# Token rows of expert slots: fetched by index in the experts' loop, not scattered beforehand

## The reference, cut to what matters

```
probs = softmax(flat @ router_w.T)                 # 4096 x 8
topk_probs, topk_idx = top_k(probs, 2)             # two experts for each token
gates = topk_probs / (sum + 1e-9)
h = silu(x @ w1[e].T) * (x @ w3[e].T)              # 341 wide, for the token's two experts
out[n] = sum over its two experts: gate * (h @ w2[e].T)
```

## Time and profile before

| | |
|---|---|
| profiled execution, its own time | 2860.51 us |
| span from first to last instruction | 2858.6 us |
| mean granted TensorE clock | 0.899 of full speed |
| TensorE busy | 2337.6 us (82%), 16656 instructions |
| GpSimd busy | 537.8 us (19%), 575 instructions |
| `route_block` | 2473.7 to 2635 us of the span |
| `experts_block` | 2636.0 to the end |

### The profile page before, as it was taken

One profiled execution on the slowest core, in us unless ns is written; L12 is line 12 of the kernel. 1 busy time (PEld: TensorE's weight loads), 2 busy tenths in 40 slices (PEclk: granted clock), 3 DMA queues, 4 the chain that ended last, 5 costly groups with the idle time before them and its releaser, 6 DMA issues. The chain is left out here.

```text
span 2858.6 us, 46600 instructions
## 1 busy us (share of the span) xinstructions
PE 2337.6 (82%) x16656; PEld 1554.2 (54%) x16656; DVE 1682.3 (59%) x3155; ACT 1215.4 (43%) x2665; POOL 537.8 (19%) x575
## 2 busy tenths in 40 slices
PE   5585867763899999799999799999899999620995
PEld 3354545542566666466566466666566665310884
DVE  4767676764366566366566365665465664550676
ACT  2343333430455555355455355555355555410442
POOL 0133333352011011011011010110010110235332
PEclk8787887885999999899999899999899999755997
DMA  2254545478647546455655465565466461431113
GB/s 94 99 212 164 189 182 196 171 284 204 138 96 145 126 97 138 106 126 109 127 125 119 91 132 125 114 130 117 105 139 125 97 145 37 127 58 52 46 52 108
DMA packets 222862, 360.74 MB, mean 126 GB/s; under 512 B 68794, under 2 KB 124701, under 8 KB 222240
## 3 DMA queue, kind: packets, MB, share of 16 engines
q1 hardware_dynamic: 218304, 349.20, 48.8%
q0 software_dynamic: 4320, 8.43, 0.9%
HBM read 229.58 MB, written 126.56 MB: 125 GB/s over the span
## 5 line engine op out<-in xcount | busy, mean ns | idle before, releaser
L1400 ACT ACTIVATE prob<-ps 128x512 f32<-128x512 f32 (+5 forms) x1600 | 636.5, 441 | 733.5 <-PE ps L1351 587.7
L1453 DVE TENSOR_REDUCE maxima<-ps 128x1 f32<-128x512 f32 (+3 forms) x768 | 387.7, 547 | 293.7 <-PE ps L1279 146.5
L1372 PE MATMUL ps<-prob,plain 128*32 128x512 f32 (+5 forms) x3200 | 512.0, 443 | 0.0
L1423 POOL TENSOR_TENSOR products<-products,sums 128x256 f32<-128x256 f32 x192 | 140.3, 731 | 1604.5 <-DVE sums L1444 1603.2
L1458 DVE TENSOR_REDUCE maxima<-ps 128x2 f32<-128x512 f32 (+1 forms) x512 | 294.2, 608 | 242.9 <-PE ps L1290 99.7
L1444 DVE RECIPROCAL sums<-sums 128x256 f32<-128x256 f32 x192 | 331.5, 1736 | 103.9 <-ACT sums L1411 103.9
L1343 PE MATMUL ps<-q1a_s,k1a_s 128*128 128x512 f32 (+3 forms) x768 | 303.4, 395 | 0.0
L1351 PE MATMUL ps<-q1b_s,k1b_s 128*128 128x512 f32 (+3 forms) x768 | 301.3, 393 | 0.0
L1372 PE MATMUL ps<-prob,v_s 128*32 128x512 f32 (+3 forms) x1536 | 284.4, 491 | 0.0
L1279 PE MATMUL ps<-k1a_s,q1a_s 128*128 128x512 f32 (+3 forms) x768 | 234.4, 375 | 2.8 <-DMA k1a_s<-k1ah_dram 2.8
L1343 PEld LDWEIGHTS ps<-q1a_s,k1a_s 128*128 128x128 f32 x768 | 147.4, 192 | 126.8 <-issue 118.9
(11 more groups left out here) (332 smaller groups left out, 4837.1 us busy)
## 6 DMA issues: line engine op xcount, KB each, us to landing
qh_dram<-pairs SPq DMA_DIRECT2D x96, 512.0 KB, 3.3
kwh_dram<-pairs SPq DMA_DIRECT2D x64, 512.0 KB, 3.0
qa_s<-qh_dram SPq DMA_DIRECT2D x128, 256.0 KB, 4.5
kwa_s<-kwh_dram SPq DMA_DIRECT2D x128, 256.0 KB, 7.4
q1a_s<-qh_dram SPq DMA_DIRECT2D x128, 256.0 KB, 4.7
qb_s<-qh_dram SPq DMA_DIRECT2D x64, 256.0 KB, 9.0
kwb_s<-kwh_dram SPq DMA_DIRECT2D x64, 256.0 KB, 9.9
k1a_s<-k1ah_dram SPq DMA_DIRECT2D x32, 512.0 KB, 6.9
```

The costliest lines, as they stand in the source:

```text
L1372: mm = pe.matmul(ps[at:at + VD, SCORES + k % 2, q0 - c * CH:q0 - c * CH + w], w_, m.prob[:, n % PROBS, h, 0:w], start=first, stop=True, sk ...
L1400: act.activation(m.prob[:, u % PROBS, h, 0:w], ps[:, turn % SCORES, 0:w], ACT.Exp, scale=SCALE).then_inc(s["exp_done"], 1)
L1423: pool.tensor_tensor(o, o, m.sums[:, br, cc], ALU.mult).then_inc(s["divided"], 1)
L1453: ins = dve.tensor_reduce(partial[:, h, i, part:part + 1], bank[:, 0:w], AX, ALU.max)
```

## The change

The place of each pair is found as before. The scatter is gone, and with it the zeros, the second copy of the tokens and the index column (rows are now 128 wide). SP stores the normalised tokens once, in token order, in eight DMAs of 256 KB as they become ready. Small tables grow by `lanes` and `edges`, and `token` holds float numbers, one more than the pair's.

What is needed instead is the inverse: for each place, its pair. The kernel forms `behind[pair, s]` = (slot of pair >= 128 s) for s = 0..71 (64 tiles of pairs, 4608 elements a partition), sums it to get the tile number and so the lane (slot mod 128), forms a one-hot `at_lane[pair, lane]`, multiplies `behind` by the pair's number, and adds up `at_lane^T x behind` over the 64 tiles on TensorE. The difference of neighbouring columns is the number of the pair at that lane of slot s. It works in four quarters of 16 tiles:

```diff
+            for q in range(QUARTERS):
+                pe.wait_ge(s["lanes_done"], q + 1)
+                pe.wait_ge(s["named_done"], q + 1)
+                for n in range(q * PAIRS_OF // QUARTERS, (q + 1) * PAIRS_OF // QUARTERS):
+                    mm = pe.matmul(ps[:, 7, 0:SLOTS + 1], at_lane[:, n % TILES_OF, :], behind[:, n, :], start=n == 0,
+                                   stop=n == PAIRS_OF - 1)
+                mm.then_inc(s["found_done"], 1)
...
             for g in range(groups):
                 act.wait_ge(s["back"], g + 1)
                 act.copy(xf[:, g * CH:(g + 1) * CH], ps[:, 2 + g % 2, :]).then_inc(s["back_copied"], 1)
+                if g == 1:
+                    act.wait_ge(s["w_loaded"], 48)
+                if g in (1, 3):
+                    k = g // 2
+                    act.copy((m.w1, m.w3)[k][0][:].rearrange("p e n -> p (e n)"), raw[k]).then_inc(s["w_hi"], 1)
...
-            pool.wait_ge(s["placed"], 1)
-            for t in range(TILES_OF):
-                for k in range(2):
-                    pool.indirect_dma_start(m.xs, bass.IndirectOffsetOnAxis(ap=where[:, k, t:t + 1], axis=0),
...
+            for k, (hi, lo) in enumerate((m.w1, m.w3)):
+                pool.wait_ge(s["w_hi"], k + 1)
+                pool.tensor_tensor(lo[:].rearrange("p e n -> p (e n)"), raw[k],
...
+            for q in range(QUARTERS):
+                pool.wait_ge(s["behind_done"], 2)
+                pool.tensor_tensor(behind[:, qq, :], behind[:, qq, :], each_tile(token[:, qq], SLOTS + 1), ALU.mult)\
+                    .then_inc(s["named_done"], 1)
+            pool.wait_ge(s["w_hi"], 3)
+            pool.tensor_tensor(m.w2[:, :, :, 1, :], raw[2].rearrange("p (e k n) -> p e k n", e=NE, k=KH),
...
```

VectorE, behind `slot` (left out between the last two: six more operations on 71 columns, which give the rows to store to, `m.put`):

```diff
+            dve.wait_ge(s["w_lo"], 2)
+            dve.tensor_tensor(behind, each_tile(slot[:], SLOTS + 1), each_token(edges[:], PAIRS_OF), ALU.is_ge)\
+            dve.tensor_reduce(tile_no[:], behind, AX, ALU.add).then_inc(s["behind_done"], 1)
+            run(dve.tensor_scalar(tile_no[:], tile_no[:], -float(P), float(P), ALU.mult, ALU.add))
+            run(dve.tensor_tensor(lane[:], slot[:], tile_no[:], ALU.add))
+            for q in range(QUARTERS):
+                if q >= 2:
+                    dve.wait_ge(s["found_done"], q - 1)
+                dve.tensor_tensor(at_lane[:, q % 2 * n:(q % 2 + 1) * n, :], each_tile(lane[:, qq], P), each_token(lanes[:], n), ALU.is_equal)\
...
+            dve.wait_ge(s["found_done"], QUARTERS)
+            run(dve.tensor_copy(found[:], ps[:, 7, 0:SLOTS + 1]))
...
+            dve.tensor_scalar(m.get[:], place_of[:], 0.0, None, ALU.max)
```

The low parts of the weights move from VectorE to GpSimd; `behind` lies in the memory of the raw weights w1 and w3, so that VectorE waits for their low parts. In the experts' block SP's loads of `xin` go, and GpSimd issues both the fetch of the rows and the store:

```diff
+            def get(g):
+                if g >= 3:
+                    pool.wait_ge(s["x_ready"], g - 2)
+                for n, i in enumerate(tiles(g)):
+                    at = bass.IndirectOffsetOnAxis(ap=m.get[:, i:i + 1], axis=0)
+                    pool.indirect_dma_start(m.xin[:, g % 3, n, :], None, m.xs, at, bounds_check=B * T - 1, oob_is_err=False)\
+                        .then_inc(s["in%d" % (g % 3)], 16)
+
+            for g in range(2):
+                get(g)
             for i in range(SLOTS):
+                if i % GROUP == 0 and i // GROUP + 2 < loads:
+                    get(i // GROUP + 2)
                 pool.wait_ge(s["y_done"], i + 1)
-                at = bass.IndirectOffsetOnAxis(ap=m.xin[:, g % 3, i % GROUP, P:ROW].bitcast(I32), axis=0)
+                at = bass.IndirectOffsetOnAxis(ap=m.put[:, i:i + 1], axis=0)
```

More of the change, by code:

```diff
@@ L1532, in route_block @@
     above = sb("above", [P, SLOTS, NE], F32)
-    slot = sb("slot", [P, 2, TILES_OF], F32)
-    where = sb("where", [P, 2, TILES_OF], I32)
+    slot = sb("slot", [P, PAIRS_OF], F32)
+    behind = raw_13[:, 0:PAIRS_OF * (SLOTS + 1)].rearrange("p (n s) -> p n s", n=PAIRS_OF)
+    tile_no, lane = [sb(n, [P, PAIRS_OF], F32) for n in ("tile_no", "lane")]
+    at_lane = t2[:].rearrange("p b (n q) -> p (b n) q", q=P)
+    lanes = sb("lanes", [P, P], F32)
+    edges = sb("edges", [P, SLOTS + 1], F32)
+    found = sb("found", [P, SLOTS + 1], F32)
+    place_of, spare = [sb(n, [P, SLOTS], F32) for n in ("place_of", "spare")]
     owner_f = sb("owner_f", [P, SLOTS], F32)
     stack = ExitStack()
-    s = open_sems(nc, stack, "w_loaded t_loaded0 t_loaded1 t_loaded2 t_loaded3 small_loaded empty_set cleared w_hi "
+    s = open_sems(nc, stack, "w_loaded t_loaded0 t_loaded1 t_loaded2 t_loaded3 small_loaded w_hi w_lo "
                              "turned t_copied stats aggregated std_done xn_done back back_copied logits_done shifted "
-                             "exp_done chosen_done counted placed scattered chain id_done copied ones_set")
+                             "exp_done chosen_done counted behind_done named_done lanes_done found_done kept chain ones_set")
     groups = TILES_OF // GROUP
@@ L1552, in _ @@
             for k, name in enumerate(("w1", "w3", "w2")):
[L1553 to L1557, removed]
+                sp.dma_start(raw[k], d[name]).then_inc(s["w_loaded"], 16)
+            for g in range(groups):
+                sp.wait_ge(s["xn_done"], GROUP * (g + 1))
+                rows = m.xs[GROUP * g * P:GROUP * (g + 1) * P]
+                sp.dma_start(rows.rearrange("(t p) n -> p t n", p=P), xn[:, GROUP * g:GROUP * (g + 1), :])\
+                    .then_inc(s["kept"], 16)
+            sp.wait_ge(s["kept"], 16 * groups)
             sp.wait_ge(s["w_loaded"], 48)
@@ L1613, in _ @@
-            pool.memset(empty[:, P:ROW].bitcast(I32), 2 * B * T).then_inc(s["empty_set"], 1)
-            pool.wait_ge(s["small_loaded"], 16 * 6)
-            for k in range(2):
[L1616 to L1620, removed]
@@ L1729, in experts_block @@
     loads = -(-SLOTS // GROUP)
-    m.xin = sb("xin", [P, 3, GROUP, ROW])
+    m.xin = sb("xin", [P, 3, GROUP, P])
     m.xh = sb("xh_t", [C, 2, CH], F32R)
@@ L1749, in tiles, with rows_in @@
         return range(GROUP * g, min(GROUP * (g + 1), SLOTS))
+    def rows_in(g):
+        return sum(len(tiles(x)) for x in range(g % 3, g + 1, 3))
     def puts_before(i, k):
@@ L1757, in _ @@
         def _(sp):
[L1758 to L1766, removed]
             for k in range(4):
@@ L1788, in turn_x @@
                 for i in range(len(tiles(g))):
-                    mm = pe.transpose(ps[:, 7, i * P:(i + 1) * P], m.xin[:, g % 3, i, 0:P], m.ident[:])
+                    mm = pe.transpose(ps[:, 7, i * P:(i + 1) * P], m.xin[:, g % 3, i, :], m.ident[:])
                 mm.then_inc(s["x_ready"], 1)
```

70 lines of the change are left out of this document (35 added, 35 removed).

## The result

The changed kernel took 2892.61 us (median of 4 runs, 2890.21 to 2895.0) against 2861.78 us (2857.88 to 2863.4) for the kernel before: ratio 1.011, 95% interval 1.0092 to 1.0127. That is slower, where 2835 us was predicted. Run again later, word for word, it took 2851.27 us (2846.49 to 2855.57) beside 2861.22 us: ratio 0.9958, interval 0.9945 to 0.9971, which is faster; and a third time 2893.7 us. The experiments show what differs between these runs; what brings the slower condition about stays open.

The account below looks back on a forecast made before the run. GpSimd's scatters and drain bound the stretch before the experts' loop, TensorE the loop. 41.3 us gained up to the first group less 15.1 in the loop gives 26.2, so 2835 us; range 2816 to 2852.

Parts of the forecast that it names:

- the ring: In the loop, fetches stand behind stores, stores behind compute, compute behind fetches: 11.3 us a group against 10.2, loop +15.1.
- the last leg: End of a loop round: the fourth fetch's landing, 2.3 us, and the semaphore, 0.05 us.
- I price no loss of clock: In the loop, TensorE's stalls of 1 us were taken to cost no clock.
- the term for the low parts of w1 and w3: Before `slot`, GpSimd takes them over from VectorE, 6.0 us for 2736 elements, done by about 2510: nothing gained.
- ScalarE's copies: Before `slot`, ScalarE copies w1 and w3 to their high parts, 2.46 us each, after waiting for weights: +2.0 us taken.
- the lock: VectorE operations of two SBUF inputs and GpSimd ones don't run together but take turns; applied to one-hots and names.
- the turns under the lock: After `slot`, names, `lane`, names and first one-hot take turns on VectorE and GpSimd: 7.8 us, 2.8 without the lock.
- a risen clock: Rival: TensorE's clock rises during the 64 products, 5 us less, 2829; chance 0.10 together with no lock.
- dear products: Rival: the 64 products after `slot` take 0.59 us each, 10.5 us more, 2845; chance 0.08.
- The sign of being wrong: From the fourth group TensorE idles about 1 us before line 1786's transposes; the prediction is wrong if that wait is missing.
- indirect reads land late: Rival: the loop's fetches land in 3.3 us, 15 rounds x 1.0 more, 2849; chance 0.15.
- fetches drawn out: Rival: GpSimd's loop fetches cost 2.9 us each beside VectorE, +7.6 in 14 rounds, about 2930; chance 0.10.

Follow-up runs that it names:

- with the lock away: Changed kernel with GpSimd's subtractions for the low parts of w1 and w3 only after VectorE has written all normalised rows: 2846.51 us.
- fetches alone: Version with one fetch before each store, but SyncE storing plainly to consecutive rows and GpSimd's fetches paced one a tile (output in wrong places): 2827.47 us.
- the spread version with the late subtractions: Changed kernel with one fetch before each store, twelve tiles ahead, five buffer groups, GpSimd's subtractions after the normalised rows: 2817.77 us, later 2875.1 us.
- stores in fours: Kernel before with its stores issued four in a row once a group is computed, eight result buffers: 2908.38 us, later 2915.66 us.

## Why the prediction was wrong

In the first run the loop took 254.7 us where the sum had 203.3. The step that failed there is the ring's first leg, "from `turn_x` to that store 3.82 us": it took 6.2 us (median of the 14 rounds) with TensorE's semaphore updates late, the last leg about 2.8 instead of 2.35, and a round 14.4 instead of 11.3. The sum has no term for updates that come late, nor for the clock ("I price no loss of clock"), which fell to a mean of 0.86; the two together make the longer leg, and no run tells them apart. The other step that failed is the term for the low parts of w1 and w3, which the sum put at nothing; it cost 7.3 us. What is left, the second run shows best.

By pieces, against the second run, whose spans differ by 2858.6 - 2850.4 = 8.2 us where 26.2 was predicted:

- *Before `slot`*, +2.0 predicted, +9.4 measured. ScalarE's copies were right: with the lock away the piece is 64.6, +2.2 (65.0 to 65.7 in the other runs without it). What failed is the sentence "Both are done by about 2510, long before `slot`". It priced GpSimd's two subtractions by their own end (they ended at 2510.8) and did not ask what VectorE does meanwhile, 7.3 us. Yet the lock was in the earlier trace rows, and the prediction used it for the one-hots. The kernel before hints at it too: its line 1648 reads 330/336/640 ns, the long ones beside GpSimd's copies.
The Trainium skill (GPSIMD Engine Reference, 8. Key points) says that GpSimd contends with VectorE instructions in a 2-port performance mode or with two SBUF inputs; the 6.13 us instruction has one tensor input, in SBUF, so this trace agrees if it runs in such a mode, which no row tells.
- *`slot` to the first transposes*, 56.2 predicted, 56.3 measured in the second run, 56.2 in the others. The sum is right; of its terms the turns under the lock took 6.5 us for 7.8, the products with their wait 28.8 for 27.3. The rivals of a risen clock (it stayed at 0.50) and of dear products (0.435 us each) fall.
- *The loop*, +15.1 predicted, 214.0 - 188.2 = +25.8 measured. The mechanism was right: moving the fetches by two stores takes it away. The size was off in each term: 3.83 for 3.82, to the fourth fetch 5.26 for 5.12, landing 2.61 for 2.3, together 11.7 for 11.3. From the fourth transposes on the 14 rounds took 167.0 us where 156.9 had been put down (13 of 11.29 and a last of 10.15); the round before them lost 1.4, not 0.9. The last did not fit (11.9): its last fetch landed after 4.1 us. Of the rounds of 12.1 to 12.7, two had a last landing of 3.0 and 3.5 us, one a second fetch issued 0.9 us late, and one a first leg of 4.35 in place of 3.83 while the granted clock was 0.50. So the sentence on the clock failed here too, at little cost: during a wait of 2.3 us it fell, for 6.8 us. (The sign of being wrong names line 1786 for these transposes; they are line 1813.) The landing was taken from the stores for want of a row; line 1919 here shows 2.4/2.6/4.5 us. So the rival "indirect reads land late" held by 0.3 of its 1.0 us.
The Trainium skill (DMA: Bandwidth & Descriptors, Anatomy of one DMA — SWDGE (gpsimd) path) has the receipt of a write heaviest for HBM, from which the prediction took that a fetch into SBUF lands sooner, if anything. Here a fetch landed in 2.6 us and a store to HBM in 2.3, so for the whole landing the measurement decides otherwise; no row shows the receipt by itself.
- *First and third run*: loops of 254.7 and 261.7 in place of 214.0. That no part of the prediction had: it is more than the ring, and the rival "fetches drawn out" forecast a slower kernel for another cause (they take 1.0 us). It was not in the trace of before, where indirect DMAs and TensorE's work are apart (scatters) or the DMAs are 2.55 us apart (stores). With it the change is slower than before, as the first result says. That the second run lies inside the range of 2816 to 2852 owes something to its width: the gain was 10 us, not 26.

Open: what sets the late updates on a given run, and by what path a burst of indirect DMAs delays TensorE's semaphores, and whether others' too. An untested rival is the recording of the profile: every trace of the sets with late updates lacks part of its records (fetches alone too), the traces of the other sets do not, and every execution here has its span and clock recorded, so that none shows a kernel without the recording. Not tried: a pace between one and two indirect DMAs a tile. Four versions that compute the whole were run in both conditions, and none of them beats the kernel before with the late updates; without them the spread version with the late subtractions does, by 1.5%.

## What to carry to other kernels

Work that is put on another engine "long before it is needed" must be checked against what the other engines do at that moment, not only against its deadline. Where one queue carries both a loop's inputs and its outputs, write down the ring (input behind output behind compute behind input) and add one step of lead; here that cost nothing and took 24 us off the loop. A design that keeps GpSimd issuing without a pause beside a busy TensorE should be timed on several chips or days before it is trusted.

## What the hardware showed beside that

- Indirect DMAs follow one another every 1.30 us on GpSimd in the loop, fetches (1001 ns) slightly longer than stores (987 ns); landing 2.6 and 2.3 us.
- A VectorE instruction of one SBUF input and 0.34 us took up to 6.13 us beside GpSimd's subtraction of 2736 elements (6.05 us, 2.21 ns an element) in the first run of the changed kernel.
- In some runs TensorE's semaphore updates come up to 5.6 us late while indirect DMAs are issued 1.3 us apart. With fetches and stores on GpSimd the loop is then 41 to 76 us longer than in the other run of the same kernel, with stores in fours alone 4 us. In the others, with the same program, every update comes within 0.02 us.
- 64 products of 72 columns, one behind the other for 13.9 us twice, left the granted clock at 0.50.
